# First layer: the buffer of decay sums loaded in four pieces along the free axis, with a semaphore each

## The reference

```python
zxbcdt = x @ W_in.T                       # gate z, xBC, dt for 64 heads
xBC = causal_conv_silu(xBC, conv_w)       # xs (512), B (128), C (128)
dt = softplus(dt_raw + dt_bias)
a = dt * -exp(A_log)
cum = cumsum(a, within a chunk of 128 tokens)
Lmat = exp(where(j <= i, cum[i] - cum[j], -inf))      # per head
M = (C[i] . B[j]) * Lmat * dt[j]
Yd = M @ xs                               # tokens of the same chunk
Yoff = exp(cum[i]) * C[i] . state_before  # tokens of earlier chunks
y = Yd + Yoff + D * xs
out = rmsnorm(y * silu(z)) * norm_w @ W_out.T
```

## Time and profile before

| | us |
|---|---|
| median of 3 runs (1801.04 to 1806.90) | 1801.53 |
| the profiled execution | 1797.77 |
| its span, from the first to the last instruction | 1796.0 |
| PE busy | 1452.3 |
| DVE busy | 912.7 |
| ACT busy | 541.2 |
| POOL busy | 336.6 |

### The profile page before, as it was taken

One profiled execution on the slowest core, in us unless ns is written; L12 is line 12 of the kernel. 1 busy time (PEld: TensorE's weight loads), 2 busy tenths in 40 slices (PEclk: granted clock), 3 DMA queues, 4 the chain that ended last, 5 costly groups with the idle time before them and its releaser, 6 DMA issues. The chain is left out here.

```text
span 1796.0 us, 22171 instructions
## 1 busy us (share of the span) xinstructions
PE 1452.3 (81%) x7452; PEld 881.9 (49%) x7452; DVE 912.7 (51%) x1942; ACT 541.2 (30%) x830; POOL 336.6 (19%) x311
## 2 busy tenths in 40 slices
PE   5968798769876987699999967877855399987997
PEld 3435544554444444566666644344444155544464
DVE  5446354535364526541311358768778544565425
ACT  1545053513442335322221223413301132122321
POOL 2125002610253025320030010000011700000024
PEclk9989699879988898999999988988975799998999
DMA  6112001200130012220000062000000200011113
GB/s 220 27 24 49 2 24 27 48 2 1 27 72 3 1 27 55 70 90 1 1 0 0 0 239 86 0 0 0 0 1 12 93 25 20 30 36 41 56 51 106
DMA packets 46785, 70.25 MB, mean 39 GB/s; under 512 B 7702, under 2 KB 38870, under 8 KB 44505
## 3 DMA queue, kind: packets, MB, share of 16 engines
q1 hardware_dynamic: 43612, 60.53, 11.6%
q0 software_dynamic: 3072, 8.39, 1.5%
HBM read 51.83 MB, written 17.08 MB: 38 GB/s over the span
## 5 line engine op out<-in xcount | busy, mean ns | idle before, releaser
L307 PE MATMUL l_b<-l_xnT,all_region_a 128*128 128x512 f32 x544 | 251.2, 612 | 14.5 <-ACTq L540 13.1
L307 PEld LDWEIGHTS l_b<-l_xnT,all_region_a 128*128 128x128 f32 x544 | 105.0, 196 | 139.6 <-issue 110.9
L653 POOL TENSOR_TENSOR all_region_b<-all_region_b,l_lc 128x512 f32<-128x512 f32 x64 | 85.9, 1377 | 355.8 <-DMA all_region_b<-l_lc_rows 355.8
L307 PE MATMUL l_b<-all_region_a,l_hT 128*128 128x256 f32 x384 | 111.1, 414 | 0.0
L817 DVE TENSOR_TENSOR l_hT<-all_region_b,l_b 128x512 f32<-128x512 f32 x48 | 33.0, 688 | 136.0 <-PE l_b L307 113.7
L1440 PE MATMUL l_banks<-l_xnT,mid_region_c 128*128 128x512 f32 (+1 forms) x192 | 93.4, 641 | 3.5 <-DVE l_xnT L1643 2.6
L1440 PE MATMUL l_banks<-mid_region_c,l_hT 128*128 128x256 f32 x192 | 55.0, 439 | 41.4 <-DVE l_hT L1612 41.4
L665 POOL TENSOR_TENSOR l_rw<-l_xdt,l_decay 128x512 f32<-128x512 f32 x64 | 70.5, 1136 | 78.5 <-DVE l_xdt L835 78.5
L307 PEld LDWEIGHTS l_b<-all_region_a,l_hT 128*128 128x128 f32 x384 | 70.5, 198 | 24.3 <-issue 15.8
L2218 POOL TENSOR_TENSOR l_rstd<-l_moments,all_neg_half 128x4 f32<-128x4 f32 x20 | 21.4, 1072 | 318.4 <-DVE l_moments L2260 318.4
L567 ACT ACTIVATE all_region_b<-all_region_b 128x512 f32<-128x512 f32 x64 | 70.0, 1094 | 4.1
(11 more groups left out here) (391 smaller groups left out, 2822.6 us busy)
## 6 DMA issues: line engine op xcount, KB each, us to landing
all_region_b<-l_lc_rows SPq DMA_DIRECT2D x64, 256.0 KB, 4.7
l_slots_in<-mid_zeros SPq DMA_DIRECT2D x1, 4992.0 KB, 23.6
mid_vector_rows<-l_slots_in SPq DMA_DIRECT2D x39, 128.0 KB, 2.1
l_slots_out<-all_region_a SPq DMA_DIRECT2D x39, 128.0 KB, 1.7
all_region_a<-l_gate_up SPq DMA_DIRECT2D x1, 4096.0 KB, 13.7
all_x<-x SPq DMA_DIRECT2D x4, 512.0 KB, 5.8
all_region_a<-w_gate_up SPq DMA_DIRECT2D x1, 2048.0 KB, 16.8
all_region_a<-l_down SPq DMA_DIRECT2D x1, 2048.0 KB, 19.0
```

What stands on the lines that cost most here:

```text
L307: return nc.tensor.matmul(out, lhsT, rhs, start=start, stop=stop, **kw)
L653: nc.gpsimd.tensor_tensor(bc[:, :, heads], bc[:, :, heads], spread(lc[:, c, heads], 1, BLK), ALU.subtract).then_inc(dd_ready.sem, 1)
```

## The change

The buffer `bc` keeps its size but has the piece as its outer axis: 4 pieces of 32 tokens x 16 heads, so that a piece is contiguous on a partition. The rows in DRAM have the same order. The store of the sums (line 288) becomes four stores, one per piece, with runs of 16 numbers in place of 64. Each chunk's loads become 16 (four pieces by four blocks), each of 2 KB to a partition in place of 8 KB. Before the loads of piece k SP waits for `e_ready` of piece k of the chunk before. Each piece has its own semaphore, and POOL waits for it in front of that piece's subtraction. POOL, ACT, DVE and PE do the same instructions in the same order, on the new layout.

```diff
--- before.py
+++ after.py
@@ -180,7 +180,7 @@
     pair = flat[:, 2 * GROUP:4 * GROUP].rearrange("p (a n) -> p a n", a=2)[:, :, 0:GT * N_EXP * N_EXP]
     gt = pair[:, 0, :].rearrange("p (t e f) -> p t e f", t=GT, e=N_EXP)
     eq = pair[:, 1, :].rearrange("p (t e f) -> p t e f", t=GT, e=N_EXP)
-    lc_d = nc.dram_tensor("l0_lc_rows", (TOKENS // GROUP, GT, P * HEADS), F32).ap()
+    lc_d = nc.dram_tensor("l0_lc_rows", (TOKENS // GROUP, PIECES, GT, P * PH), F32).ap()
     yg = sb("yg", [P, Z_BLK, P])
     ysq = sb("ysq", [P, Z_BLK, P])
 
@@ -217,7 +217,7 @@
     a_ready = Event(sem("l0_a_ready"), 1)
     lc_ready = Event(sem("l0_lc_ready"), 1)
     lc_out = sem("l0_lc_out")
-    bc_landed = sem("l0_bc_landed")
+    bc_landed = [sem(f"l0_bc_landed{k}") for k in range(PIECES)]
     dd_ready = Event(sem("l0_dd_ready"), NCH * PIECES)
     decay_ready = Event(sem("l0_decay_ready"), 3)
     bc_ready = Event(sem("l0_bc_ready"), NCH)
@@ -285,16 +285,19 @@
         sp.dma_start(l1.out, io["w_attn_outT"].rearrange("(k p) n -> p k n", p=P)).then_inc(l1.sem, 16)
         for g in range(TOKENS // GROUP):
             sp.wait_ge(lc_ready.sem, lc_ready.done(g))
-            sp.dma_start(lc_d[g].rearrange("c (p h) -> p c h", p=P), lc[:, :, :]).then_inc(lc_out, 16)
-            sp.wait_ge(lc_out, 16 * (g + 1))
+            for k in range(PIECES):
+                sp.dma_start(lc_d[g, k].rearrange("c (p h) -> p c h", p=P), lc[:, :, k * PH:(k + 1) * PH]).then_inc(
+                    lc_out, 16)
+            sp.wait_ge(lc_out, 16 * PIECES * (g + 1))
             for c in range(NCH):
                 n = g * NCH + c
-                if n > 0:
-                    sp.wait_ge(e_ready.sem, e_ready.done(0, n * PIECES - 1))
-                for q in range(NB):
-                    rows = lc_d[g, c].rearrange("(q n) -> q n", q=NB)[q:q + 1, :].broadcast_to([BLK, BLK * HEADS])
-                    sp.dma_start(bc[q * BLK:(q + 1) * BLK, :, :].rearrange("p i h -> p (i h)"), rows).then_inc(
-                        bc_landed, 16)
+                for k in range(PIECES):
+                    if n > 0:
+                        sp.wait_ge(e_ready.sem, e_ready.done(0, (n - 1) * PIECES + k))
+                    for q in range(NB):
+                        rows = lc_d[g, k, c].rearrange("(q n) -> q n", q=NB)[q:q + 1, :].broadcast_to([BLK, BLK * PH])
+                        sp.dma_start(bc[q * BLK:(q + 1) * BLK, k, :, :].rearrange("p i h -> p (i h)"), rows).then_inc(
+                            bc_landed[k], 16)
         last = TOKENS // GROUP - 1
         sp.wait_ge(up_b.filled.sem, up_b.filled.done(last, 5))
         sp.dma_start(l1.w1, io["w1T"].rearrange("(k p) n -> p k n", p=P)).then_inc(l1.sem, 16)
@@ -559,7 +562,7 @@
                 def exps(c, k):
 
                     n = c * PIECES + k
-                    part = bc[:, :, k * PH:(k + 1) * PH]
+                    part = bc[:, k, :, :]
                     act.wait_ge(dd_ready.sem, dd_ready.done(g, n))
                     nc.scalar.activation(part, part, ACT.Relu, scale=-1.0)
                     act.drain()
@@ -647,10 +650,10 @@
 
                 def differences(c):
 
-                    pool.wait_ge(bc_landed, 16 * NB * (g * NCH + c + 1))
                     for k in range(PIECES):
                         heads = slice(k * PH, (k + 1) * PH)
-                        nc.gpsimd.tensor_tensor(bc[:, :, heads], bc[:, :, heads], spread(lc[:, c, heads], 1, BLK),
+                        pool.wait_ge(bc_landed[k], 16 * NB * (g * NCH + c + 1))
+                        nc.gpsimd.tensor_tensor(bc[:, k, :, :], bc[:, k, :, :], spread(lc[:, c, heads], 1, BLK),
                                                 ALU.subtract).then_inc(dd_ready.sem, 1)
 
                 def weigh(c):
@@ -2660,7 +2663,7 @@
     l1.qkv = take(3 * DK, DIM)
     l1.out = take(DK, DIM)
     mem.l0_e = take(4, 512).rearrange("p a (h i) -> p a h i", h=16)
-    mem.l0_bc = take(32, HEADS)
+    mem.l0_bc = take(4, 512).rearrange("p a (i h) -> p a i h", h=16)
     l1.w1 = mem.region_a[:, 0:DK * FFN_BLK * P].rearrange("p (a b) -> p a b", a=DK)
     at = DK * (D_IN + N_EXP)
     l1.w2 = mem.region_a[:, at:at + FFN_BLK * DIM].rearrange("p (a b) -> p a b", a=FFN_BLK)
```

## The result

The changed kernel takes 1782.1 us in the median of 4 runs (1772.43 to 1791.45), against 1801.53 before (also 4 runs, 1801.04 to 1806.90). The ratio is 0.9876, with a 95% interval of [0.9828, 0.9923]. So it is faster by 19.4 us where 35.9 were forecast, and the time lies above the range. The profiled execution took 1786.36 us, 11.4 less than that of before; its span is 1784.6.

The account below looks back on a forecast made before the run. PE was taken as the bound, stalled by the chain Exp, load, POOL, ACT, copy. Gains of 29.3 + 7.1 + 3.0 less costs of 2.4 + 1.2 gave 35.9 us, so 1765.6 at the median; range 1755 to 1777.

Parts of the forecast that it names:

- Part 1: PE's wait for ACT's copy before each group's first assembly goes, as pieces load early: 29.3 us gained.
- L: Time from an Exp's end to POOL's subtraction of the reloaded piece: 3.8 us forecast, 7.52 before; above 4.7 PE waits.
- Parts 2 and 5: PE leaves the stall at high clock, gaining 7.1 us; POOL's weighing for chunk 1 ends about level, costing 1.2.
- the 1 us: Sign of error: POOL's weighing (line 665) releases PE by more than 1 us.
- Part 3: Two small PE waits before the assembly of chunk 2, in groups 2 and 3, go: 3.0 us gained.
- case (d): Rival: clock falls in a group's last chunk, in no group (1756) or all four (1776), 10 us; within 0.78.
- Part 4: POOL's subtractions of chunk 1 lengthen DVE's mask products in chunk 0: 0.6 us a group, 2.4 in all.
- the 1.2: Sign of error: DVE's product with the mask grows past 1.2 us in chunk 0.
- Part 6: SP's 16 loads a chunk take 6.7 us against 17.5, and the row store is covered: no cost counted.
- (a): Rival: pieces land no sooner than the whole, PE still waits 2.8 us; gain 23 us, 1778.5; chance 0.13.
- (b): Rival: SP's issuing of loads becomes the bound; at 1.5 us an issue, 1844 us; chance 0.04.
- (c): Rival: another wait, such as for POOL's weighing, replaces the stall; only 3.0 us gained, 1798.5; chance 0.05.

Follow-up runs that it names:

- e12: Kernel before, with the masked C.B in PSUM and PE's wait before a group's first assembly filled by seven repeated down products: 1790.96 us, ratio 0.9931.
- e6: Changed kernel, with PE's short waits for DVE filled by computing the down products there two or three times: 1771.63 us, ratio 0.9805.
- e1: The changed kernel measured again without any edit, against the kernel before: 1785.96 us, ratio 0.9875.
- e5: Changed kernel, with the masked C.B in PSUM in place of SBUF, down products rotating over two banks: 1762.64 us, ratio 0.9749.
- e7: Kernel before, with the masked C.B in PSUM in place of SBUF, down products rotating over two banks: 1794.00 us, ratio 0.9915.
- e11: Kernel before, with PE's wait before a group's first assembly filled by seven more down products: 1799.81 us, ratio 0.9969.

## Why the prediction was wrong

**Part 1, the stall: right.** Forecast -29.3, measured -28.8. L was forecast at 3.8 us; for the first piece it is 3.3 (Exp ends at 113.2, subtraction at 116.56) and for piece 2 it is 5.3 (116.55 to 121.82), since the 16 issues took 8.72 us, one of them 1.87. That is above the 4.7 at which a wait was to come back, and yet PE waits for 0.33 us only, as Exp(0,2) ended 0.7 us sooner than in the trace of before; that is luck, and the margin of the step was smaller than it said. By the step's own chain the copy starts 3.0 us after piece 2's subtraction (117.2 + L to 120.2 + L): 121.8 + 3.0 = 124.8, and it stands at 124.82.

**Parts 2 and 5, the clock behind the stall and `weigh(1)`: right together.** Forecast -7.1 and +1.2, so -5.9; measured -5.5. The 1.04 us before `l_rw` in group 0 is the second term, and it is over the 1 us that the prediction had named as a sign of being wrong. e12 adds a caution that the prediction lacked: this gain is PE's only because the same change frees the chain of the copy.

**Part 3: the waits went, the gain didn't.** They are 0.6 us in the sum, as forecast, but the distance in which they lay is 2.8 us longer. There the clock is low. The windows of PE after (stretch, length, busy, granted clock, DMA share, GB/s), to set beside the earlier trace rows:

```profile
142.00:146.00 4.00, 3.86 (x17) 0.73 0.12 28
166.00:170.00 4.00, 4.00 (x31) 0.50 0.00 0
```

The output projection at 143.57 takes 3.53 us, against 1.97 at the high clock. PE came from two waits of 2.64 and 1.30 us. At the high clock throughout, piece 3 to assembly takes 4.48, 4.48 and 4.07 us in chunks 1 to 3, 52.1 in all. After, the sum is 68.3, so 16.2 us are lost in this way; before it is 65.5, of which 3.0 are part 3's waits, so 10.4 were lost. That is the prediction's case (d), and its size, +5.8, is within the 10 given; its cause, new short waits, wasn't named. e6 shows it: with the waits filled the sum is 53.6. The size is that of one execution: in e1, the same kernel, the sum is 65.7, which leaves 3.2 us missing here and not 5.8.

**Part 4, what moves onto DVE's time: this is the step that failed.** It said that POOL's subtractions of chunk 1 move beside DVE's work of chunk 0, and took 0.6 us a group, 2.4 in all, with 1.9 a group as the most. Measured is +18.1, an error of 15.7. Chunk 0 itself cost 4.0, at most 1.9 in a group. Its products reach 1.58 us in groups 2 and 3, past the 1.2 that the prediction had named as a sign of being wrong. The rest, 15.2 less 1.0 in chunk 3, is in chunks 1 and 2, which the step didn't look at: POOL waited 4.91 and 6.72 us for the load before the subtractions of chunks 2 and 3 too, so these moved as well, from 144.88 to 130.67 and from 164.16 to 151.74, onto DVE's add and the product for piece 2, and `weigh`, for which the step had no price at all, meets the product for piece 3. The prediction had even said that POOL would wait less than 1 us there, and didn't ask on whose time it would then work. The two meetings cost 1.06 us (1.75 in place of 0.69) and 0.88 (1.57), one after another on the path: 1.9 us a chunk, eight chunks.

The rule of the Trainium skill that was weighed (SBUF — State Buffer, section SBUF: two separate sides), that a VectorE operation with two SBUF inputs and a GpSimd operation exclude each other, is borne out: products of 1.75 us beside subtractions of 1.27, and none over 0.690 in e5, where one input is in PSUM. It was set aside for a longest product of 1.66 us in the trace before. That maximum, at 730.09, stands beside a `weigh` that starts at 730.10 and is 0.97 longer than the median, a meeting of the same kind; it was read as a bound on a rare meeting, not as the price of each. The price worked out from the rule, 10.7 us, was laid on chunk 0 and the subtractions alone, so it too falls short of the 18.1.

**Part 6 and the rivals.** SP's 8.72 us for 16 issues (6.7 forecast) are hidden, as is the row store. (a) didn't come true: the first piece has an L of 3.3 us and a 64 KB load lands in 2.0. The Trainium skill's rule to coalesce small transfers (DMA: Bandwidth & Descriptors, section Rules for kernel authors) was no guide here, since the consumer works in pieces and the issues are hidden. (b) and (c) didn't come true either. The row store of group 1 is issued 4.2 us sooner (258.8 against 263.0), not 9.

**The sum.** In the profiled execution 24.5 us are missing: 15.7 in part 4, 5.8 in the clock, 0.9 in parts 1, 2 and 5, and 2.0 in places that I didn't trace further. By the medians 16.5 us are missing; the profiled execution was one with more of the slow clock than the median (its time is 4.3 us above it). With the products' contention taken out of both kernels, the change gains 31.4 us (e7 to e5), near the 35.9.

Left open: in e5 the slow clock came in chunk 3 of every group and I can't say why there. No run changes `weigh` alone; its share is read from the products that stand beside it. Most of the 14 us of e7 aren't placed either.

## What to carry to other kernels

When a load is released sooner, the engine behind it starts sooner in every trip of the loop: lay its moved work, for each trip and not only for the one with the stall, beside the timelines of the other engines, and look for operations there on which the bounding engine waits. Count every operation of that engine, not only the one whose input came sooner: here the products beside `weigh` lost 10.4 us, and the products and adds beside the subtractions 12.5. A maximum of 1.66 us over a median of 0.69 is the price of one meeting; count the meetings after the change. Where two elementwise engines have to meet, put one operand of the critical one in PSUM, and where TensorE is left with waits of 1 to 3 us in a row, try whether repeating a product in them pays.

## What the runs showed of the hardware

- A fp32 product of 128x512 on DVE with both operands in SBUF takes 0.69 us alone and up to 1.76 beside POOL in the changed kernel; with one in PSUM, 0.672 to 0.690 in all 64 (e5). POOL pays as well: its subtraction has a median of 1.28 us and takes up to 1.79.
- DVE can wait through more than one POOL operation. In e11 two such products, started while `weigh` was running, took 3.29 and 3.40 us and ended 0.55 us after the last of its four products. `weigh` itself took 4.17 us both times, no longer than in the kernel before:

```profile
693.97 3.40 DVE L854 TENSOR_TENSOR all_region_b<-all_region_b,l_cbd 128x512 f32<-128x512 f32 x1
```

```profile
692.65 4.17 POOL L666 TENSOR_TENSOR l_rw<-l_xdt,l_decay 128x512 f32<-128x512 f32 x4
```

- 64 KB broadcast loads land in 2.0 us (1.8 to 3.5), 256 KB ones in 4.7. A store of 32 KB with runs of 64 bytes lands in 1.9 us, where one of 128 KB with runs of 256 took 2.0.
- Computing a down product again (some 0.9 us a round), up to two more times where PE would have waited, made the changed kernel faster by 13 us (e6): the mean granted clock of the span rose from 0.895 to 0.909.
